# Reordering the LayerNorm epilogue, the expert dispatch and the projection stages of an eight-core attention + soft-MoE kernel, with tracked activation-table loads

## What is computed

```python
q, k, v = [gelu(x @ W1 + b1) @ W2 + b2  for each of q, k, v]
scores  = tril(q @ k.T) / scale            # no softmax: linear attention
att     = layernorm(scores @ v) * ln_w + ln_b
x1      = layernorm(x + att)
xn      = layernorm(x1) * gamma + beta     # soft-MoE input
logits  = l2norm(xn) * scale @ l2norm(mu)  # 16 experts x 16 slots
slot_in = softmax over tokens(logits).T @ xn
h       = gelu(slot_in @ w1 + b1);  slot_out = h @ w2 + b2
x2      = layernorm(x1 + softmax over slots(logits) @ slot_out)
```

## Time and profile before

| | |
|---|---|
| times of two runs | 5786.69 and 5944.38 us, median 5865.54 us |
| the profiled execution | 5785.62 us; span 5784.1 us on the slowest core |
| cores | 5765.0 to 5784.1 us, mean granted TensorE clock 0.751 to 0.757 |
| busy, share of the span | TensorE 2964.3 us (51%), ScalarE 1847.7 us (32%), VectorE 1344.2 us (23%), POOL 173.9 us (3%) |
| activation-table loads | 132, 169.4 us in all |

### The profile page before, as it was taken

The page is one execution under the profiler, slowest core; times in us unless marked ns, Lnnn a source line. Parts: engine busy times, 40 slices in busy tenths (PEclk is TensorE's granted clock), DMA queues, the critical chain, the costliest instruction groups (busy, mean ns, idle before and its releaser), DMA issues.

```text
span 5784.1 us, 40206 instructions; the slowest of 8 cores (5765.0 to 5784.1 us)
## 1 busy us (share of the span) xinstructions
PE 2964.3 (51%) x11945; PEld 1191.0 (21%) x11945; DVE 1344.2 (23%) x2022; ACT 1847.7 (32%) x3575; POOL 173.9 (3%) x299
## 2 busy tenths in 40 slices
PE   0007565656565665657565757565656561522211
PEld 0003222222222222222222222222222220100000
DVE  0000222222222222131313222222222223033333
ACT  0002333342424242424242434333342433122222
POOL 1000000000000000000000000000000000000000
PEclk9999787878787777878787878787877785555555
DMA  9995031212121121212021212020212100322222
GB/s 113 117 116 130 24 88 35 78 49 63 49 63 63 49 78 38 78 34 92 19 92 35 77 35 91 20 92 34 78 42 69 49 27 24 114 71 77 77 77 72
DMA packets 228023, 379.68 MB, mean 66 GB/s; under 512 B 78786, under 2 KB 96210, under 8 KB 226402
## 3 DMA queue, kind: packets, MB, share of 16 engines
q1 hardware_dynamic: 210738, 287.39, 15.8%
q0 software_dynamic: 17072, 89.71, 9.6%
HBM read 352.46 MB, written 101.19 MB: 78 GB/s over the span
## 4 chain that ended last, share of the span: by engine, by line
PE 40%; ACT 19%; DVE 16%; issue 11%; another core or an unknown queue 5%; DMA 4%; SPq 3%; DVEq 1%; ACTq 1%; POOL 1%; POOLq 0%
PE pSA L444 10%; PE pSB L444 8%; ACT st L71 5%; ACT jb L71 4%; DVE st L71 3%; DMA exp_in<-expb 3%; DVE slot_in L71 3%; PE pAT L535 3%; ACT tA L71 3%; PE pSA L582 2%; SPq L391 2%; DVE tB L71 2%; PE pSA L456 2%; PE pSB L582 2%
## 5 line engine op out<-in xcount | busy, mean ns | idle before, releaser
L444 PE MATMUL pSA<-x_fm,wbufA 128*128 128x512 bf16 x1536 | 409.2, 415 | 767.0 <-ACT hbuf L71 593.0
L71 DVE SCALAR_TENSOR_TENSOR st<-st 128x1 f32<-128x1 f32 x256 | 56.1, 219 | 1583.5 <-ACT st L71 980.2
L444 PE MATMUL pSB<-x_fm,wbufA 128*128 128x512 bf16 x1536 | 389.3, 399 | 0.0
L444 PEld LDWEIGHTS pSA<-x_fm,wbufA 128*128 128x128 bf16 x1536 | 155.9, 103 | 984.1 <-issue 832.6
L444 PE MATMUL pSA<-hbuf,wbufB 128*128 128x512 bf16 x1024 | 291.8, 436 | 83.2 <-ACT k_fm L71 66.2
L1197 PE MATMUL pTR<-identS,exp_in 128*128 128x128 bf16 x128 | 23.8, 289 | 536.8 <-DMA exp_in<-expb 536.8
L444 PE MATMUL pSB<-hbuf,wbufB 128*128 128x512 bf16 x1024 | 257.1, 396 | 0.0
L71 ACT ACTIVATE st<-st 128x1 f32<-128x1 f32 (+1 forms) x1024 | 225.2, 220 | 96.8 <-ACT st L71 3.6
L71 ACT ACTIVATE jb<-xn_bf 128x1024 bf16<-128x1024 bf16 x64 | 67.6, 1057 | 516.7 <-DVE xn_bf L71 513.8
L456 PE MATMUL pSA<-wbufB,hbuf 128*128 128x512 bf16 x512 | 145.8, 437 | 127.8 <-ACT v_tm L71 112.1
L444 PEld LDWEIGHTS pSB<-x_fm,wbufA 128*128 128x128 bf16 x1536 | 158.7, 103 | 210.1 <-issue 51.2
(11 more groups left out here) (160 smaller groups left out, 4597.2 us busy)
## 6 DMA issues: line engine op xcount, KB each, us to landing
wbufA<-wb SPq DMA_DIRECT2D x48, 2048.0 KB, 9.1
wbufB<-wb SPq DMA_DIRECT2D x48, 2048.0 KB, 8.9
OUT<-out_sb SPq DMA_DIRECT2D x64, 512.0 KB, 3.5
xb<-x POOLq DMA_DIRECT2D x1, 16384.0 KB, 158.9
x_tm<-xb SPq DMA_DIRECT2D x16, 1024.0 KB, 5.6
xprime<-xp_t POOLq DMA_DIRECT2D x64, 256.0 KB, 2.5
xp_in<-xprime POOLq DMA_DIRECT2D x64, 256.0 KB, 2.9
w1eb<-w1e POOLq DMA_DIRECT2D x1, 8192.0 KB, 85.2
```

The lines of the kernel that those rows point to most:

```text
L71: return s.inc(f(*a, **k))
L444: mm = t.matmul(p[:, :], wbuf[:, kc, m * 128:(m + 1) * 128], src[:, kc, :], start=(kc == 0), stop=(kc == NCH - 1))
```

## The change

The order of block b becomes: O tiles 0 and 1; e1 of pair 01; O tiles 2 and 3; x_fm load; nv1; S0; a1, e34; first half of S1 (g0 to g3); e5, nv2; second half of S1; a2, spill, nv3; S2; a3, e9, a4; ffn 0; ffn 1; pair 23 e1, nv1; S3; a1; first half of S4; e34, e5; second half of S4; nv2, a2; first half of S5; spill, nv3; second half of S5; a3, e9; kT; AT; a4; scast; supd; x_tm load; ffn 2; ffn 3. To allow the halves, `emit_stage` takes a part, and the position of each evacuation is kept in `evac_pos`; what a group waits for stays the same. `pin_act` is taken out of the steps. `EMIT` loads a table only where the class of the next step (G for Gelu, L for Ln/Exp, N for neither) differs from the set that is loaded. That makes 93 loads in the program.

```diff
-            emit_xfm(b + 1)
-            emit_stage(b + 1, 0)
-        emit_ffn(0)
-        emit_ffn(1)
...
+            emit_xfm(b + 1)
+            crun(c01, 2, 4)
+            EMIT("G", lambda: emit_stage(b + 1, 0))
+            crun(c01, 4, 8)
+            EMIT("N", lambda: emit_stage(b + 1, 1, 0))
+            crun(c01, 8, 12)
+            EMIT("N", lambda: emit_stage(b + 1, 1, 1))
+            crun(c01, 12, 18)
+            EMIT("G", lambda: emit_stage(b + 1, 2))
+            crun(c01, 18, 24)
+            EMIT("L", lambda: emit_ffn(0))
+            EMIT("L", lambda: emit_ffn(1))
+            crun(c23, 0, 4)
+            EMIT("N", lambda: emit_stage(b + 1, 3))
+            crun(c23, 4, 6)
+            EMIT("G", lambda: emit_stage(b + 1, 4, 0))
+            crun(c23, 6, 10)
+            EMIT("G", lambda: emit_stage(b + 1, 4, 1))
+            crun(c23, 10, 14)
+            EMIT("N", lambda: emit_stage(b + 1, 5, 0))
+            crun(c23, 14, 18)
+            EMIT("N", lambda: emit_stage(b + 1, 5, 1))
+            crun(c23, 18, 22)
             emit_kT(b + 1)
             emit_AT(b + 1)
-            for s in c23[20:]:
-                s()
+            crun(c23, 22, 24)
+            scast_seg(b, 0, 4)
+            scast_seg(b, 4, NCH)
             for s in supd_segs(b + 1):
                 s()
+            emit_xtm(b + 1)
...
+    def EMIT(cls, fn):
+        if cls == "G" and act_state[0] != "G":
+            emit_pin_sec(SET_GELU)
+            act_state[0] = "G"
+        elif cls == "L" and act_state[0] != "L":
+            emit_pin_sec(SET_LNEXP)
+            act_state[0] = "L"
+        fn()
```

More of the change, by code:

```diff
@@ L424, in emit_stage, with _ @@
                 dst, func, bias, scl = v_tm, AF.Identity, None, 1.0
+            lo, hi = 4 * pt, 4 * pt + 4
+            for m in range(lo, hi):
+                evac_pos[(G, m)] = A.n + (m - lo) + 1
             @block.tensor
-            def _(t, G=G, s_idx=s_idx, wbuf=wbuf, src=src, bb=bb):
+            def _(t, G=G, s_idx=s_idx, wbuf=wbuf, src=src, bb=bb, lo=lo, hi=hi):
                 W(t, "t", wsem_for(G), 16 * (G // 2 + 1))
[L429 to L442, removed]
+                if lo == 0:
+                    W(t, "t", d_fm)
+                    W(t, "t", d_c)
+                    W(t, "t", V, v_after_sadd[bb - 1] if bb > 0 else v_prologue)
+                for m in range(lo, hi):
+                    if m < 2:
+                        if s_idx in (1, 3, 5):
+                            W(t, "t", A, evac_pos[(G - 1, 7)])
+                        elif s_idx > 0:
+                            W(t, "t", A, evac_pos[(G - 1, 6 + m)])
+                    else:
+                        W(t, "t", A, evac_pos[(G, m - 2)])
+                    p = pSA if m % 2 == 0 else pSB
+                    if s_idx < 5:
                         for kc in range(NCH):
@@ L445, in _ @@
                                           src[:, kc, :], start=(kc == 0), stop=(kc == NCH - 1))
[L446 to L454, removed]
+                    else:
+                        ti, dvh = divmod(m, 2)
                         for kc in range(NCH):
@@ L491, in emit_stage, with emit_pin_sec, _, stage_cls @@
             scalar_section(f_evac)
-            stage_evac_end[G] = A.n
-            if s_idx == 5:
-                a_stage_end[bb] = A.n
+            assert A.n == evac_pos[(G, hi - 1)], (G, lo, A.n, evac_pos[(G, hi - 1)])
+            if hi == 8:
+                stage_evac_end[G] = A.n
+                if s_idx == 5:
+                    a_stage_end[bb] = A.n
+    act_state = ["L"]
+    def emit_pin_sec(set_id):
+        @block.scalar
+        def _(sc):
+            pin_act(sc, set_id)
+    def EMIT(cls, fn):
[6 more added lines that the diff above has]
+        fn()
+    def stage_cls(s_idx):
+        return "G" if s_idx in (0, 2, 4) else "N"
     emit_xtm(0)
```

97 lines of the change are left out of this document (36 added, 61 removed).

## The result

| | before | after |
|---|---|---|
| median time | 5791.74 us (10 runs, lowest 5781.66) | 6052.74 us (13 runs, lowest 5970.16) |
| ratio after / before | | 1.0377, 95% interval [1.0336, 1.0417] |
| mean block period, core 0 | 276.5 us (275.6 to 277.4) | 290.4 us (284.6 to 298.9) |
| mean block period, core 3 | 276.5 us (275.5 to 277.4) | 289.6 us (286.7 to 293.5) |
| activation-table loads | 132 | 93 |

The account below looks back on a forecast made before the run. TensorE, busy 51%, was bound by waits, the largest 34.5 us in S0. +13.5 us a block x 15 = +202, less 4 for the last block, on 5785.6 gave 5984 us; range 5900 to 6025, with rivals 5880 to 6080.

Parts of the forecast that it names:

- The walk: The new block followed stage by stage through the written order: 290.0 us against 276.5, +13.5 a block; chance 0.73.
- The nine waits: TensorE's forecast waits in S1 (two), S2, ffn 0, S4 (two), S5, k transposes and adds to S, 3.2 to 14.8 us each.
- The signs named for the walk: In the profile after: 93 loads, about 13 us wait in S4, 8 in S2, 15 ahead of ffn 0, period 290.
- the three that would have made it wrong: e34 of pair 23 starting before S4's first evacuations end, ffn 0 waiting under 10 us, or period under 282.
- The two parts of the sum: Per block, TensorE's waits grow from 66 to 74 us, 8 more; lower-clock restarts and colder ffn 0 add about 5.5.
- a fixed price for each restart: Two groups behind a wait taken as 5.8 us, between 3.5 at full clock and 6.3.
- The clock rival: S1, S4, S2, S5: clock never recovers between waits, more groups run slow; +6.5 us a block, 6080 us; chance 0.10.
- e34 isn't late: S4: VectorE starts e34 with a1's end, TensorE restarts 8.9 us earlier; 5851 us; chance 0.09.
- Both e34 covered: S1 and S4: e34 hidden beside four groups, waits of 5.1 and 12.8 us go; -9.1 a block, 5645 us; chance 0.05.
- Costed at nothing: Weight loads, the x_tm load and the xprime and exp stores arrive in time; a late one costs its lateness.
- Table loads: Loads fall from 132 to 93, counted where they stand at 1.3 us; the skill's 2.66 us would give 5964 us.

Follow-up runs that it names:

- e1: Kernel before with S0 of the next block written behind nv1 of pair 01, ahead of the rest of its epilogue: ratio 1.0057, mean period 280.1 us.
- e4: Kernel after with the 8 CASTs of S written back ahead of S3, no longer ahead of the adds: ratio 0.9975, median 5793.41 us.
- e3: Kernel after with e34 of pair 23 written ahead of the first half of S4: profiled execution 5835.83 us beside 5797.57 before, mean period 279.7 us.
- e6: Kernel after with a1 and e34 of pair 01 written ahead of S0: ratio 1.0099, mean period 280.3 us.
- e2: Kernel before with table loads tracked and nothing moved, 95 loads instead of 132: ratio 1.0036.
- e9: Kernel after with e34 of pair 23 ahead of S4, CASTs beside S3, and a1 and e34 of pair 01 ahead of S0, together: ratio 0.9563.
- e10: Kernel after with finer epilogue pieces in another order, one tile at a time, both a1 of each pair first: ratio 0.8782, median 5100.13 us.
- e8: Kernel after with 4 of the 8 CASTs back beside S3: profiled execution 5943.67 us beside 5793.95 before, mean period 287.2 us.

## Why the prediction was right, point by point

**The walk.** Forecast +13.5 us a block, measured +13.2 on core 3 (+13.9 on core 0 with its stretches at 0.81); forecast 5984 us, measured 6004 by the ratio and 5970 in the shortest execution. The nine waits, in order, against the forecast: S1 3.2 (3.2) and 5.7 (5.1), S2 8.5 (8.2), ffn 0 14.8 (14.8), S4 3.6 (4.4) and 12.3 (12.8), S5 5.4 (6.2), the k transposes 11.4 (10.9), the adds 6.1 (6.3). They sum to 71.0 against 71.9. In the next block, 2914.3 to 3198.9 us, which has no time at 0.81, they are 3.2, 5.7, 8.2, 14.8, 4.3, 13.1, 6.2, 11.1 and 6.5, 73.1 in all. Each one of them was worked out from what stands ahead of it in ScalarE's and VectorE's written order, with durations of before. The signs named for the walk were there, and none of the three that would have made it wrong: e34 started behind the evacuations, ffn 0 waited 14.8 us, and no block of core 0 or core 3 was under 284.6.

**The two parts of the sum.** Forecast were 8 us of waits and 5.5 of lower clock; measured on core 3 are 8.1 and 5.1. For the waits this is more than the number, since each came out singly. For the clock part it is partly luck. The walk made of it a fixed price for each restart, and with prices of that kind the expectation for e1 was 4.8 us a block too high, and that for e4 (6 to 7.7 less) fell short of the 13.1 measured. e1 kept a wait of 44.6 us and cost 3.6 us a block; e4 took 8 us of stretch away and gave 13.1. So the price holds in the kernel after and isn't a constant.

**The clock rival** (0.10) fell. Its +6.5 us a block on top of the walk are reached by no block of core 3, where the longest is 3.9 above the mean. On core 0 the blocks of 295.7 and 298.9 us reach it, but by their 76 and 78 us at a granted clock of 0.81, which is not the rival's mechanism. By that mechanism the clock would stay low between the two waits of a stage. Between those of S1 it did not: from 2673 to 2678 us the granted clock was 1.00, with TensorE busy 4.4 of the 5 us.

**e34 isn't late** (0.09) fell by the row at 2783.55. **Both e34 covered** (0.05) fell by the two waits of 5.7 and 12.3 us; e3 and e6 show that its gain was real, 9.9 and 9.3 us a block, and where the steps would have had to be written for it.

**Costed at nothing.** The weights came in time: no wait of TensorE in the block is for a DMA. **Table loads:** e2, in which 37 loads less gave no gain, bears out that they count by where they stand; the prediction's sum took the measured 1.3 us, and in after the next ACTIVATE again starts 1.30 us after a load (2774.08 to 2775.38).

**Which part did it.** Of the three places tried, no one is the cause. Put back singly, e34 of pair 23 gives 9.9, a1 with e34 of pair 01 9.3 and the CASTs 13.1 us a block, 32.3 together and more than twice the loss of 13.2. At once, in e9, they give 289.6 - 259.8 = 29.8, nearly their sum. So the gain of the removed 34.5 us wait was there, and these three places, with the new wait ahead of ffn 0, gave it back. The wait ahead of ffn 0 was changed by itself in no run.

## What to carry to other kernels

In a program of hand-written streams where a step waits for all that is written ahead of it, moving a large piece out of one wait helped here only once its steps were written right behind their own data, ahead of unrelated work on the engine that releases them. Walk the written order of each engine with durations from the trace, and the waits come out to within 1 us, as they did here. Cut foreign work on the evacuating engine into small pieces: in e10, with pieces of up to about 4.3 us beside a lead of two groups of 1.73 us, no wait for hbuf was over 2.8 us. Judge a change of waits by the block period, and read the granted clock of each block beside it, since taking a stall of the adds away gave 0.7 times its length (e8) or 1.6 times (e4) here. Compare blocks, and cores, at the same levels of the clock: a stretch at 0.81 made some blocks of core 0 longer for a reason outside their waits.
